# Half-tile banks for the transposed scores, a third bank for the maxima, and a later batch's maximum begun at step 7

## What is computed

```python
x = _layernorm(x + attn(x, ...))                     # one head, causal
q = shape(x @ wq, T); k = shape(ctx @ wk, S); v = shape(ctx @ wv, S)   # H = 16, dh = 8, T = 56, S = 1500
scores = jnp.einsum('bhtd,bhsd->bhts', q, k) + bias  # bias depends on s - t, constant beyond a distance
weights = jax.nn.softmax(scores, axis=-1)
x = _layernorm(x + (jnp.einsum('bhts,bhsd->bhtd', weights, v) ...) @ wo)
x = _layernorm(x + ffn(x, ...))                      # five matmuls, SiLU gate and two exact GELUs
```

## Time and profile before

| what | value |
|---|---|
| median of 3 runs | 1088.15 us (1086.52 to 1097.75) |
| the profiled execution: its own time | 1093.1 us |
| its span, first to last instruction | 1091.3 us |
| mean granted TensorE clock | 0.952 of 2.4 GHz |
| the exponential L769, 128x896, mean of one | 925 ns |
| one reduction L108, mean | 683 ns |
| key load / query load, issue to landing, median | 6.2 / 6.4 us |

### The profile page before, as it was taken

How to read it: one execution, slowest core, us unless ns; L and a number is a source line. 1 busy time by engine, 2 the same in 40 slices (tenths; PEclk the granted TensorE clock), 3 DMA queues, 4 the chain that set the end, 5 groups by cost and what they waited for, 6 DMA issues and landing times. The chain is left out here.

```text
span 1091.3 us, 25611 instructions
## 1 busy us (share of the span) xinstructions
PE 969.3 (89%) x10410; PEld 657.2 (60%) x10410; DVE 721.8 (66%) x1510; ACT 605.5 (55%) x1071; POOL 421.6 (39%) x418
## 2 busy tenths in 40 slices
PE   6754579999999999999999999989999988799996
PEld 3542256666666666666666666666666666545564
DVE  6565447878778877878778878876777774540014
ACT  2321157666667666666666666666666656352232
POOL 7330535554444555554444555554444400000000
PEclk9866689999999999999999999998999999899999
DMA  7507665555666655555665755554665420300000
GB/s 228 192 10 163 117 190 178 164 177 178 191 177 204 185 176 179 163 178 178 191 194 161 209 179 177 164 179 147 188 181 162 137 78 2 109 1 1 1 9 25
DMA packets 57388, 156.10 MB, mean 143 GB/s; under 512 B 23936, under 2 KB 36152, under 8 KB 54200
## 3 DMA queue, kind: packets, MB, share of 16 engines
q1 hardware_dynamic: 56744, 152.85, 48.1%
q10 hardware_dynamic: 528, 1.63, 0.4%
HBM read 111.63 MB, written 42.63 MB: 141 GB/s over the span
## 5 line engine op out<-in xcount | busy, mean ns | idle before, releaser
L769 ACT ACTIVATE e_sb<-st_ps 128x896 f32<-128x896 f32 (+1 forms) x384 | 354.1, 925 | 153.0 <-DVE st_ps L714 93.5
L108 DVE TENSOR_REDUCE cmax<-max_ps 112x1 f32<-112x512 f32 x512 | 337.6, 683 | 150.5 <-PE max_ps L98 150.4
L98 PE MATMUL max_ps<-kst,qst 111*112 111x512 bf16 x760 | 283.8, 401 | 37.8 <-PEq L117 14.1
L611 PEld LDWEIGHTS st_ps<-qst,kst 114*128 114x128 bf16 (+1 forms) x3072 | 191.7, 101 | 88.7 <-issue 41.8
L821 POOL TENSOR_TENSOR kpart<-k_left,kpart 128x500 bf16<-128x500 f32 x90 | 102.7, 1141 | 352.4 <-ACT k_left L787 347.8
L611 PE MATMUL st_ps<-qst,kst 114*128 114x112 bf16 (+1 forms) x3072 | 215.7, 213 | 19.5 <-DMA qst<-nmp 18.3
L105 DVE CUSTOM_DVE_ANT_0 near_out<-max_ps,near_nat 112x476 bf16<-112x476 f32 x248 | 154.0, 649 | 26.4 <-PE max_ps L98 26.4
L98 PEld LDWEIGHTS max_ps<-kst,qst 111*112 111x112 bf16 x760 | 92.2, 130 | 106.8 <-DVE cmax L108 38.9
L641 PE MATMUL pv_ps<-e_sb,vals 128*32 128x168 f32 (+1 forms) x3072 | 150.0, 313 | 0.3 <-ACT e_sb L769 0.3
L685 PEld LDWEIGHTS misc<-wv,ctxt 128*128 128x128 f32 (+1 forms) x768 | 99.6, 193 | 15.8 <-ACT vals L754 11.8
L641 PEld LDWEIGHTS pv_ps<-e_sb,vals 128*32 128x32 f32 (+1 forms) x3072 | 80.4, 109 | 47.1 <-issue 34.6
(11 more groups left out here) (127 smaller groups left out, 941.1 us busy)
## 6 DMA issues: line engine op xcount, KB each, us to landing
kst<-kparts SPq DMA_DIRECT2D x192, 375.0 KB, 6.2
kparts<-kpart SPq DMA_DIRECT2D x90, 375.0 KB, 2.7
ctxt<-in_ctxT SPq DMA_DIRECT2D x32, 750.0 KB, 7.4
qst<-qslots SPq DMA_DIRECT2D x192, 28.0 KB, 6.4
qslots<-qst SPq DMA_DIRECT2D x4, 672.0 KB, 11.2
kparts<-kst SPq DMA_DIRECT2D x6, 375.0 KB, 3.1
h<-in_h SPq DMA_DIRECT2D x2, 1024.0 KB, 8.6
qst<-nmp SPq DMA_DIRECT2D x96, 1.8 KB
```

Source lines behind the costliest of these rows:

```text
L98: return nc.tensor.matmul(dst[0:TT, 0:hi - lo], m.qst[0:M_ROW, r, p, :], m.kst[0:M_ROW, r, p, lo:hi], start=True, stop=True)
L108: return nc.vector.tensor_reduce(m.cmax[:, r, c, p:p + 1], src[0:TT, 0:BOUND[c + 1] - BOUND[c]], AX.X, ALU.max)
L611: mm = nc.tensor.matmul(st_ps[0:K, j % 2, p // 4, (p % 4) * TT:(p % 4 + 1) * TT], m.kst[0:AUG, u % RING, p, j * P:j * P + K], m.qst[0:AUG, ...
L769: nc.scalar.activation(e_sb[0:K, j % E_RING, :].rearrange("p (a c) -> p a c", a=2), st_ps[0:K, j % 2, :, 0:HALF], ACT.Exp).then_inc(s_ex, 1)
```

## The change

Scores are made, near-biased and exponentiated in halves of 4 pairs (448 columns), one bank each, in a ring of three banks: half w = 2(12b + j) + h waits for the exponential of half w-3. The maxima get a ring of three banks (n waits for n-3), and the scratch output of L105 too. `HEAD_START` becomes 10, so `M0` becomes 7 and `NM` (the step of the final maximum) 6. Semaphore counts of `s_st`, `s_ex` and `s_nb` double.

```diff
-HEAD_START = 8
+HEAD_START = 10
+ST_BANKS, MAX_BANKS = 3, 3
...
-            out=m.near_out[:, p % 2, :], in0=src[0:TT, 0:FIRST_CH], in1=m.near_nat[:, p, :],
+            out=m.near_out[:, p % MAX_BANKS, :], in0=src[0:TT, 0:FIRST_CH], in1=m.near_nat[:, p, :],
...
-        max_ps = ctx.enter_context(nc.psum_tensor("max_ps", [P, 2, 512], F32))
-        st_ps = ctx.enter_context(nc.psum_tensor("st_ps", [P, 2, 2, 512], F32))
+        max_ps = ctx.enter_context(nc.psum_tensor("max_ps", [P, MAX_BANKS, 512], F32))
+        st_ps = ctx.enter_context(nc.psum_tensor("st_ps", [P, ST_BANKS, 512], F32))
...
-                wait(pe, s_ex, batch(g, u) * ST + j - 1)
                 K = st_rows(j)
-                for p in range(PAIRS):
-                    mm = nc.tensor.matmul(st_ps[0:K, j % 2, p // 4, (p % 4) * TT:(p % 4 + 1) * TT],
...
-                mm.then_inc(s_st, 1)
+                for h in range(2):
+                    w = 2 * (batch(g, u) * ST + j) + h
+                    wait(pe, s_ex, w - ST_BANKS + 1)
+                    for p in range(4):
+                        mm = nc.tensor.matmul(st_ps[0:K, w % ST_BANKS, p * TT:(p + 1) * TT],
...
+                    mm.then_inc(s_st, 1)
...
-                wait(pe, s_mr, batch(g, u + lag) * CHUNKS + n - 1)
-                max_scores(nc, m, max_ps[:, n % 2, :], r, c, p).then_inc(s_mx, 1)
+                wait(pe, s_mr, batch(g, u + lag) * CHUNKS + n - MAX_BANKS + 1)
+                max_scores(nc, m, max_ps[:, n % MAX_BANKS, :], r, c, p).then_inc(s_mx, 1)
...
-                wait(pe, s_ex, n * ST + t + 2)
+                wait(pe, s_ex, 2 * (n * ST + t + 2))
...
-                        dve.wait_ge(s_st, b * ST + j + 1)
...
-                        nc.vector.tensor_tensor(t, t, near, ALU.add).then_inc(s_nb, 1)
+                        for h in range(2):
+                            w = 2 * (b * ST + j) + h
+                            dve.wait_ge(s_st, w + 1)
+                            if j == 0:
+                                t, near = st_ps[:, w % ST_BANKS, 0:HALF], m.near_t0[:, h * HALF:(h + 1) * HALF]
...
+                            nc.vector.tensor_tensor(t, t, near, ALU.add).then_inc(s_nb, 1)
...
-                        w = b * ST + j
-                        if j < 2:
-                            act.wait_ge(s_nb, 2 * b + j + 1)
-                        act.wait_ge(s_st, w + 1)
                         wait(act, s_pv, b * PAIRED + j // 2 - 1)
-                        nc.scalar.activation(e_sb[0:K, j % E_RING, :].rearrange("p (a c) -> p a c", a=2),
-                                             st_ps[0:K, j % 2, :, 0:HALF], ACT.Exp).then_inc(s_ex, 1)
+                        for h in range(2):
+                            w = 2 * (b * ST + j) + h
+                            if j < 2:
+                                act.wait_ge(s_nb, 4 * b + 2 * j + h + 1)
+                            act.wait_ge(s_st, w + 1)
+                            nc.scalar.activation(e_sb[0:K, j % E_RING, h * HALF:(h + 1) * HALF],
+                                                 st_ps[0:K, w % ST_BANKS, 0:HALF], ACT.Exp).then_inc(s_ex, 1)
...
-                    wait(sp, s_st, b * ST)
+                    wait(sp, s_st, 2 * b * ST)
```

24 lines of the change are left out of this document (11 added, 13 removed).

## The result

The changed kernel takes 1094.46 us (median of 20 runs, of which 19 lie between 1082.23 and 1097.5), the kernel before 1087.69 us (20 runs, 1084.61 to 1097.75). The ratio of the means, 1093.10 to 1088.16 us, is 1.0045, with a 95% interval of 1.0026 to 1.0064: slower by a little under half a per cent, about 5 us (the medians lie 6.8 us apart), where 0.4% faster was forecast. The profiled execution took 1093.73 us. Ratios leave out runs over 1.5% above the fastest of their kernel: here one at 2295.17 us, and four of the ten with matmuls behind the wait, further down.

What follows compares the result with a forecast made beforehand. GpSimd's order and two DMA latencies were taken to keep the time; -5.6 + 4.5 - 0.5 - 1.8 - 0.5 = -3.9 us on the profiled 1093.1 gave 1089.2, or 1084.2 us at the median; range 1067 to 1102 us.

Steps and rivals of the forecast that it cites:

- the mechanism of the loop: Repeated batches: first scores, step 4's key projection, GpSimd's splits, maxima and their DMA close a 24.51 us loop; -0.2 us a batch.
- The stretch from step 7 to the next first scores: End of a batch: 8.49 us less 0.38 of DMA wait and 1.0 of bank waits, 7.1 us.
- Waits at step 7: The maxima at step 7 would wait for the query DMA in over half the batches, 0.3 to 1 us each.
- the waits behind VectorE: TensorE's waits for VectorE to free a bank of maxima would fall from 63 us to under 20.
- the batch before the last: No key work there, so maxima a step sooner would gain 1.8 us (0 to 1.9).
- The rival in which TensorE sets the pace: Whole loop: TensorE's own waits bound the kernel, so 42 us would go, giving 1046 us; chance 0.12.
- The load did become the bound: Rival: if step 7 to next first scores takes 8.1 us, late landings cost 18 us; priced at 1101 us; chance 0.20.
- the sum for late loads: Step 7 in repeated batches: six query landings past 17.2 us would cost 4.5 us in all (0 to 18).
- The last batch: ScalarE's first half ready after 0.61 us instead of 1.10 would gain 0.5 us (-0.6 to +0.7).
- the rival of the interlocking halves: Steps 1 to 4: second halves wait 0.2 us each for the exponential before, 0.8 a batch; 1112 us at median; chance 0.10.
- The estimate from the Trainium skill: ScalarE's 12 added exponentials would cost 1.7 us a batch, hidden in 28 batches and visible in the last.

Runs made afterwards that it cites:

- matmuls behind the wait: Changed kernel with four added matmuls, their result overwritten, placed after the wait for the queries at step 7: ratio 1.0094 to the kernel before.
- the case of the moved product: Changed kernel with key loads issued part by part, and GpSimd's reciprocal product moved behind the maxima's subtractions, its reader two steps later: 1075.29 us, ratio 0.9814.
- the second trace of before: The kernel before run once more with no edit: 1089.91 us beside 1088.37, ratio 1.0001.
- the kernel with work ahead of the wait: Changed kernel with four added matmuls (14 in batch 29), result overwritten, ahead of step 7's wait for the queries: 1083.51 us, ratio 0.996 to the kernel before.
- earlier loads: Changed kernel with each part of the keys loaded when its own store has ended, not after the last store: 1083.06 us, ratio 0.9899 to the kernel before.

## Why the prediction failed, by its own steps

What it said of the mechanism of the loop came true. The period of the repeated part was to be 24.3 and is 24.25; -0.2 us a batch was taken and 0.25 measured, -7.0 for -5.6 us over the loop. Some of that fit is luck: the forecast had the halves only as a cost of 0 to 0.25 us a batch, and they brought 0.12 of the gain. The stretch from step 7 to the next first scores was to be 7.1 us and is 24.25 - 17.19 = 7.06 in batch 3, whose queries land at 17.15. Waits at step 7 were to come in over half of the batches (20 of 29, but of up to 4.4 us and not 0.3 to 1), the waits behind VectorE to fall under 20 us (16.0), the batch before the last to gain 1.8 (2.0). The rival in which TensorE sets the pace is refuted for this kernel (period not under 23.8, GpSimd without a gap) and the case of the moved product shows GpSimd's order as the bound. The halves do not interlock in the loop, as long as the near-bias add comes in time. The load did become the bound, in single batches, but not in the way that rival was priced: the stretch of 7.1 us never grew to 7.8.

The step that failed is the sum for late loads: "The six late ones exceed it by 5.1 us in all, of which two already cost 0.6 today: +4.5 us". It priced a late load at its lateness. In batches 1 to 28 of the changed kernel late loads cost 10.9 us over 28 x 24.25, beside 1.9 in the second trace of before: +9.0, twice the term. Three batches, 7, 10 and 21, account for the gap: by landing + 7.06 they should take 25.22, 24.70 and 25.31 us and took 27.10, 26.82 and 26.86, 5.6 us more in all. Without those 5.6 the term would be +3.4. They are the price of the half clock behind a stop of some 2 us, which the forecast did not have among its costs; the pair of batches above shows it, and the kernel with work ahead of the wait takes it away and its ratio falls by 0.85%.

The trace of before had this price in it, behind another wait. The longest wait for queries in its loop was 0.8 us, but the DMA of the maxima was late twice; the longest wait of that group in the earlier trace rows is such a stop, and this is the batch behind it:

```profile
737.45 0.93 PE L611 MATMUL st_ps<-qst,kst 114*128 114x112 bf16 x8 [2.52 <-DMA qst<-nmp]
...
737.45:764.61 27.16, 26.06 (x300) 18.30 (x300) 19.15 (x39) 16.91 (x30) 11.74 (x13) 0.89 0.47 138
```

The stop itself lies in the batch ahead of this one; this one takes 27.16 us instead of 24.51 at a mean clock of 0.89, 2.6 us for the clock alone. Behind the other, of 1.64 us, a batch took 25.90 at 0.93, 1.4 us. In the second trace of before the batch behind such a stop kept its clock and took 24.50. The working took the late landings, three of them 2.0 to 2.6 us behind the new step 7, moved the reader 1.9 us forward, and never asked what such stops do to the engine behind them.

Two terms outside the loop failed as well:
- Batch 29 was in the sum only as one of the six late landings, 17.80 us, at 0.6 us: its own shape was given no price. It has no key projection, so TensorE reaches step 7 at 13.16 us instead of 15.71, and waits 4.58 us for queries that land at 17.70. By landing + 7.06 it would take 24.8; with the clock at 0.50 in the windows from 879.8 to 883.8 it took 27.06: +3.1 us, of which 2.3 are put down to the clock. With this batch the late loads cost 12.1 us more than before, beside the +4.5. With earlier loads (landing at 13.65) batch 29 takes 20.93.
- The last batch was to gain 0.5 and lost 1.3. ScalarE's timeline there:

```profile
918.86 1.85 ACT L775 ACTIVATE e_sb<-st_ps 128x448 f32<-128x448 f32 x4 [0.41 <-PE st_ps L614]
921.13 1.85 ACT L775 ACTIVATE e_sb<-st_ps 128x448 f32<-128x448 f32 x4 [0.42 <-PE st_ps L614]
```

The same in the kernel before:

```profile
918.34 3.52 ACT L769 ACTIVATE e_sb<-st_ps 128x896 f32<-128x896 f32 x4
922.12 3.51 ACT L769 ACTIVATE e_sb<-st_ps 128x896 f32<-128x896 f32 x4 [0.27 <-PE st_ps L611]
```

Every two tiles ScalarE waits 0.41 us for scores, which before came 0.27 us late once in four. The halves are the cause: from the first scores to the end of the last exponential this batch takes 14.93 us after the change and also with the halves and two banks of maxima, and 13.40 with whole tiles and the early maximum (13.40 and 13.61 in the two traces of before). It is the rival of the interlocking halves, at the one place where nothing covers them. That three half banks hold less than two whole tiles is the likely reason; no run tries four. The split itself costs little: four halves take 1.85 us where two whole exponentials are 1.76 and four 3.52. The estimate from the Trainium skill, "VectorE: DVE Perf Modes", section on the TRN2 errata, spoke against splitting (1.7 us more in the last batch) and lies near the loss, but these rows don't bear out its reason: the halves follow each other by 0.46 us and the idle time is a wait for TensorE.

The sum, redone with what was measured, against the second trace of before: loop -7.0, batch 0 -0.7, late loads +9.0, late DMAs of the maxima +3.1 (two in this trace, one in that), batch 29 +3.1, batch 30 -2.0, last batch +1.3, both ends -0.9: +5.9 us, which is the table's +5.8 with rounding. The late DMAs of the maxima come in both kernels and are no part of the change as far as these runs show.

What stays open. Whether a given stop lowers the clock was not predictable from its length alone: 6 of 13 waits of 1.9 to 2.2 us did, and the trace with matmuls behind the wait had three waits of 2.3 to 2.9 us, read the same way, and no fall. That the latest landings come from one store of key parts that takes over 4 us instead of 2.6 is in the traces; why that store takes so long was not found, nor why the DMA of the maxima is late by 1 to 2 us at batches 23 and 26 in several traces. And the kernel with the moved product, the fastest here that computes everything, still has late loads to be removed, and a near-bias add that its reader delays.

## What to carry to other kernels

Price a late transfer not by its lateness alone: when it stops TensorE for 2 us, the matmuls behind it may run at half the clock, here 1.5 to 2.9 us more for each half clock that came, and a few matmuls put ahead of the wait bought them back. Look for that price behind any long stop of the engine in the trace that you have, not only behind the wait that you are about to lengthen. Before moving a first reader forward, lay the landings of its operands beside the new time, for every batch and the odd ones (here the first without key work), and move the loads first. Where equal periods repeat with no engine full, look for the engine whose fixed order holds the loop: moving one 0.66 us operation behind three small ones gained 0.85%, nearly as much as the new banks and the removal of late loads together (1.0%, on another chip). And when an operation moves, its reader moves in another engine's order: look at what then stands behind it there.

## What the runs showed of the hardware that was not expected

- A stop of TensorE that long: of 125 waits in twelve traces none of the 60 under 1 us was followed by a fall of the granted clock from 1.00 to 0.50, 11 of 12 between 2.2 and 3.0 us were. The Trainium skill, "TensorE: Matmul & The Clock Gate", section "HAM oscillation — how this bites in real kernels", tells of a kernel in which the clock falls when TensorE waits for DMAs; the traces agree, with 27.10 us for a batch that lateness alone would make 25.2.
- Of two batches with the same late queries (18.42 and 18.37 us) and about the same stop, the one whose clock stayed at 1.00 took 25.53 us and the one whose clock fell 28.26.
- Two subtractions of 8x112 elements took VectorE 1.09 and 1.18 us beside GpSimd's splits, where GpSimd does each in 0.39; the price on the whole kernel was 5.4%.
- A store of one key part takes 2.5 us at least, 2.7 in the median and 5.9 at most, on one and the same queue with the same bytes:

```profile
L869 SPq DMA_DIRECT2D kparts<-kpart x90: 319/326/1112, 137.9 to 862.9; - x90
...
DMA to landing us min/median/max: 2.5/2.7/5.9
```

(duration of the issue in ns, minimum, median, maximum; below it the time from issue to landing). A kernel whose loop has a slack of 0.7 us has to be laid out for the longest of them.
